# Expert routing moved from a stage of its own into the loop of the memory attention

## The reference

```python
def _L0_ffn_ref(x, router_w, w1, b1, w2, b2):       # E = 8 experts, C = 1536 places each
    logits = x_flat @ router_w.T
    probs = softmax(logits)
    chosen_e, chosen_p = argmax(probs), max(probs)
    onehot = one_hot(chosen_e, E)
    pos = cumsum(onehot, axis=0)[token, chosen_e] - 1     # over all 8192 tokens, in order
    kept = pos < C
    buf[chosen_e, clip(pos)] += x_flat * kept             # then the experts' two products on buf
    y = eo[chosen_e, clip(pos)] * chosen_p * kept
x = x + _L0_xattn_ref(_layernorm(x), ctx_1024, ...)   # "memory attention": 16 heads of 64,
                                                      # keys of 128 tokens and 77 memories
x = x + _L0_ffn_ref(_layernorm(x), ...)
```

## Time and profile before

| | us |
|---|---|
| median of 3 runs (lowest, highest) | 3627.68 (3622.21, 3630.70) |
| the profiled execution: its own time | 3633.43 |
| its span, from the first to the last instruction | 3631.6 |
| busy in the span: PE, DVE, ACT, POOL | 3202.6, 2524.3, 2207.0, 1508.8 |
| mean granted clock of PE | 0.929 of full |

### The profile page before, as it was taken

One profiled execution on the slowest core, in us unless ns is written; L12 is line 12 of the kernel. 1 busy time (PEld: TensorE's weight loads), 2 busy tenths in 40 slices (PEclk: granted clock), 3 DMA queues, 4 the chain that ended last, 5 costly groups with the idle time before them and its releaser, 6 DMA issues. The chain is left out here.

```text
span 3631.6 us, 96279 instructions
## 1 busy us (share of the span) xinstructions
PE 3202.6 (88%) x27249; PEld 2343.7 (65%) x27249; DVE 2524.3 (70%) x7783; ACT 2207.0 (61%) x8571; POOL 1508.8 (42%) x2416
## 2 busy tenths in 40 slices
PE   8999999899999999999999731887996999977776
PEld 4656565788888888888888520665664666644444
DVE  7888888676777777777767640114666888879997
ACT  6888888566666666666666300334776999962221
POOL 6888888111111111111111125004654777746665
PEclk9999999999999999999999855999998999986666
DMA  4000000000000000000000101321000000000000
GB/s 138 0 0 0 0 0 1 4 2 3 2 2 2 2 2 2 2 2 2 2 2 2 70 9 50 84 77 30 17 16 5 6 5 5 6 3 6 12 12 18
DMA packets 80357, 54.27 MB, mean 15 GB/s; under 512 B 24801, under 2 KB 74413, under 8 KB 80160
## 3 DMA queue, kind: packets, MB, share of 16 engines
q1 hardware_dynamic: 76192, 45.27, 4.4%
q0 software_dynamic: 4096, 8.16, 0.8%
HBM read 32.67 MB, written 20.97 MB: 15 GB/s over the span
## 5 line engine op out<-in xcount | busy, mean ns | idle before, releaser
L785 DVE COPY b_prT<-b_tr 128x512 f32<-128x512 f32 x512 | 352.4, 688 | 324.3 <-PE b_tr L694 320.6
L930 POOL TENSOR_TENSOR b_ln_var<-b_ln_mean_var,all_eps 128x1 f32<-128x1 f32 x64 | 12.2, 190 | 1158.5 <-DVE b_ln_mean_var L129 1158.5
L883 ACT ACTIVATE b_pr<-b_sc,b_low 128x205 f32<-128x205 f32 x1024 | 431.2, 431 | 40.9 <-DVE b_low L761 40.9
L467 ACT ACTIVATE a_pr<-a_sc,a_low 128x128 f32<-128x128 f32 x1024 | 365.5, 384 | 36.4 <-POOL a_pn L511 26.2
L776 DVE TENSOR_SCALAR b_pn<-b_pr,b_rec 128x205 f32<-128x205 f32 x1024 | 291.6, 327 | 54.7
L694 PE MATMUL b_tr<-all_ident,b_pn 128*128 128x128 f32 x2048 | 322.4, 280 | 6.2 <-DVE b_prT L785 2.5
L2064 ACT ACTIVATE f_pr<-f_sc,f_low 128x77 f32<-128x77 f32 x1024 | 320.3, 338 | 10.2 <-DVE f_low L1955 2.9
L502 POOL TENSOR_TENSOR a_kx<-a_qk,w_hsel 128x512 f32<-128x512 f32 x256 | 291.8, 1151 | 2.4 <-DVE a_qk L338 2.4
L694 PEld LDWEIGHTS b_tr<-all_ident,b_pn 128*128 128x128 f32 x2048 | 226.5, 141 | 92.2 <-issue 69.5
L254 PE MATMUL a_sc<-a_kx,a_qk 128*128 128x512 f32 x512 | 261.9, 593 | 0.0
L761 DVE TENSOR_REDUCE b_low<-b_sc 128x4 f32<-128x820 f32 x256 | 256.3, 1001 | 6.0 <-PE b_sc L682 6.0
(11 more groups left out here) (290 smaller groups left out, 8651.3 us busy)
## 6 DMA issues: line engine op xcount, KB each, us to landing
scratch_x<-r_zeros SPq DMA_DIRECT2D x12, 512.0 KB, 5.0
e_xr<-scratch_x SPq DMA_DIRECT2D x24, 256.0 KB, 3.0
scratch_y<-e_yr SPq DMA_DIRECT2D x24, 256.0 KB, 2.4
all_X<-in_x SPq DMA_DIRECT2D x8, 512.0 KB, 7.0
e_w<-in_e_w SPq DMA_DIRECT2D x16, 256.0 KB, 3.0
out_x<-all_X SPq DMA_DIRECT2D x8, 512.0 KB, 3.2
w_mask<-in_mask SPq DMA_DIRECT2D x1, 2464.0 KB, 9.8
b_cT<-in_ctxT SPq DMA_DIRECT2D x32, 77.0 KB, 1.9
```

The lines of the kernel that those rows point to most:

```text
L467: op = act.activation(pr[:, u % 2, g], sc[:, u % 2, 128 * g:128 * g + 128], ACT.Exp, bias=low[:, u % 2, g:g + 1], scale=-1.0, accum_out=su ...
L785: dve.tensor_copy(prT[:, j % 2, i].rearrange("p h t q -> p (h t q)"), tr[:]).then_inc(prT_made, 1)
L883: op = act.activation(pr[:, j % 2, g, 0:KN], sc[:, j % 2, h, KN * i:KN * i + KN], ACT.Exp, bias=low[:, j % 2, g:g + 1], scale=-1.0, accum_ ...
```

## The change

The routing's stage is gone. Its work is done inside the memory attention, for two sequences at a time, some steps behind them. The expert stage itself is the same. What is added to the loop, by engine:

- DVE: after the residual of sequence b - 1 its statistics (part 1) and its normalised rows into XN (part 2), in every step. In odd steps `find_least` (end of part 1) and `choose` (end of part 3) for sequences b - 3 and b - 2; in even steps `settle` (end of part 1) for b - 4 and b - 3.
- PE: four kinds of chunks in the ring. Even sequences' chunks get lg (logits of two sequences); odd ones get place (counts, in bf16) and two rT (transposes of XN). The ring has now 14 and 12 chunks, and xT of an even sequence stands ahead of mk2.
- ACT: the copies of those chunks, and `weigh`, two exponentials with their sums, in odd steps.
- POOL: in every step the root of the routing's norm; in even steps a wait for `settle` and two indirect DMAs.
- SP: the twelve stores of zeros stand between the first and the second load of the context.

The loop's body is four steps instead of two (`over_fours`), since the four slots of XN and the two halves of `put` go round with four sequences. After the last step the last four sequences are routed in straight code.

```diff
-        CHUNKS = [[("mk", 0), ("mk", 1), ("mk", 2), ("mk", 3), ("xT", 0), ("q", 0), ("k", 0), ("q", 1), ("k", 1),
-                   ("mv", 0), ("v", 0), ("v", 1), ("mv", 1)],
-                  [("xT", 0), ("q", 0), ("k", 0), ("q", 1), ("k", 1), ("mv", 0), ("v", 0), ("v", 1), ("mv", 1)]]
-        EARLY = [[[0, 1], [3, 4, 5], [7], [10]], [[0], [], [4], []]]
-        LATE = [[[2], [6], [8, 9], [11, 12]], [[1], [2, 3], [5, 6], [7, 8]]]
+        CHUNKS = [[("mk", 0), ("mk", 1), ("xT", 0), ("mk", 2), ("lg", 0), ("mk", 3), ("q", 0), ("k", 0), ("q", 1),
+                   ("k", 1), ("mv", 0), ("v", 0), ("v", 1), ("mv", 1)],
+                  [("xT", 0), ("q", 0), ("place", 0), ("k", 0), ("q", 1), ("k", 1), ("mv", 0), ("v", 0), ("v", 1),
+                   ("mv", 1), ("rT", 0), ("rT", 1)]]
+        EARLY = [[[0, 1], [4, 5, 6], [8], [11]], [[0], [], [5], []]]
+        LATE = [[[2, 3], [7], [9, 10], [12, 13]], [[1, 2], [3, 4], [6, 7], [8, 9, 10, 11]]]
...
 PE
+                def router_logits(n, dst):
+                    if due(n):
+                        pe.wait_ge(pj_copied, n)
+                    for i in range(2):
+                        last = pe.matmul(dst[:, E * i:E * i + E], rT[:, i], rwT[:], start=True, stop=True)
+                def count(s, dst):
+                    pe.wait_ge(choosing, 4 * s + 8)
+                    pe.wait_ge(placing, 3 * s)
+                    pe.matmul(dst[:, 0:2 * E], ones_bf[:], earlier[:].unsqueeze(1).broadcast_to([128, 2, E]), start=True, ...)
+                    pe.matmul(dst[:, E:2 * E], ones_bf[:], one_hot[:, 0], start=False, stop=False)
+                    return pe.matmul(dst[:, 0:2 * E], tri_bf[:], one_hot[:]..., start=False, stop=True)
...
 DVE
+                def choose(s):
+                    dve.wait_ge(weighed, s + 2)
+                    dve.tensor_reduce(top[:], hit[:], AX.X, ALU.max).then_inc(choosing, 1)
+                    dve.wait_ge(choosing, n + 1)
+                    dve.tensor_tensor(hit[:], hit[:], per_token(top), ALU.is_equal).then_inc(choosing, 1)
+                    dve.wait_ge(choosing, n + 2)
+                    dve.tensor_tensor(hit[:], hit[:], per_expert(rank), ALU.mult).then_inc(choosing, 1)
+                    dve.wait_ge(choosing, n + 3)
+                    dve.tensor_reduce(best[:], hit[:], AX.X, ALU.max).then_inc(choosing, 1)
+                    dve.reciprocal(chance[:], total[:]).then_inc(choosing, 1)
+                    dve.wait_ge(choosing, n + 5)
+                    dve.tensor_tensor(one_hot[:], hit[:], per_token(best), ALU.is_equal).then_inc(choosing, 1)
+                    dve.tensor_tensor(chance[:], chance[:], top[:], ALU.mult).then_inc(choosing, 1)
+                    dve.wait_ge(choosing, n + 7)
+                    dve.tensor_tensor(both[:], one_hot[:, 0], one_hot[:, 1], ALU.add)
+                    dve.tensor_tensor(chosen_base[:], one_hot[:], per_expert(base), ALU.mult).then_inc(choosing, 1)
+                def settle(s, h, copied):      # nine instructions, four waits for the one before, then put
...
                     for j in range(NJ):
+                        if j == 1 and inside(b - 1):
+                            dve.wait_ge(y_added, b)
                         copy_probs(b, j, 0)
+                        if j == 1 and inside(b - 1):
+                            route_statistics(b - 1, 1 - p)
...
                             divide(nb, nj, 1)
-                        if j == 0 and not (isinstance(b, int) and b == 0):
-                            residual(b - 1)
+                        if inside(b - 1):
+                            if j == 0:
+                                residual(b - 1)
+                            if j == 1:
+                                dve.wait_ge(r_seen, b)
+                            if j == 2:
+                                route_normalise(b - 1, (r + 3) % 4)
+                        if routed and p == 1 and j == 1:
+                            find_least(b - 3, ...)
+                        if routed and p == 1 and j == 3:
+                            choose(b - 3)
+                        if routed and p == 0 and j == 1:
+                            settle(b - 4, r // 2, chunk_end(b + 1, 1, "place", 0))
+                        if inside(b - 1):
+                            if j == 1:
+                                dve.bn_aggr(r_mv[:, 1 - p], r_stats[:, 1 - p]).then_inc(r_moments, 1)
...
 ACT, part 3 of odd steps, ahead of copy_out
+                def weigh(s):
+                    for i in range(2):
+                        act.activation(hit[:, i], minus[:, i], ACT.Exp, bias=least[:, i:i + 1], scale=-1.0,
+                                       accum_out=total[:, i:i + 1]).then_inc(weighed, 1)
...
 POOL
                     add_bias(b)
                     if not isinstance(b, int) or b + 2 < B:
                         both_norms(b + 2, p)
+                    if routed and p == 0:
+                        pool.wait_ge(placing, 3 * b - 6)
+                    if inside(b - 1):
+                        route_norm(b - 1, 1 - p)
+                    if routed and p == 0:
+                        scatter(r // 2)
...
 SP
                 load(0)
+                sp.wait_ge(zeroed, 3)
+                for n in range(rows.shape[0]):
+                    sp.dma_start(rows[n], zeros[:]).then_inc(buf_zeroed, 16)
                 with sp.Fori(1, B // 2) as j:
                     load(j)
```

More of the change, by code:

```diff
@@ L84, in over_sequences, with over_fours @@
         step(b, b % 2, b == n - 1)
+def over_fours(eng, step, n, head, tail):
+    for b in range(head):
+        step(b, b % 4)
+    with eng.Fori(head // 4, (n - tail) // 4) as j:
+        for r in range(4):
+            step(4 * j + r, r)
+    for b in range(n - tail, n):
+        step(b, b % 4)
 def wait_for_loads(nc, loaded, pairs):
@@ L720, in project_out, with step @@
                     last.then_inc(y_made, 1)
-                def step(b, p, last):
-                    first = isinstance(b, int) and b == 0
+                def step(b, r):
+                    p = r % 2
+                    first, last = isinstance(b, int) and b == 0, isinstance(b, int) and b == B - 1
+                    half = ((r + 2) % 4) // 2
                     for j in range(NJ):
@@ L751, in _ @@
                 score(0, 0, 1)
-                over_sequences(pe, step)
+                over_fours(pe, step, **steps)
+                for i in range(1, 6):
+                    after(i)
             @block.vector
@@ L800, in step @@
+                def step(b, r):
+                    p = r % 2
+                    last = isinstance(b, int) and b == B - 1
                     ahead = not isinstance(b, int) or b + 2 < B
+                    routed = not isinstance(b, int) or b >= 3
                     for j in range(NJ):
@@ L920, in _ @@
                 exponentials(0, 0, 1)
-                over_sequences(act, step)
+                over_fours(act, step, **steps)
+                for i in range(1, 5):
+                    after(i)
+                weigh(B - 2)
+                after(5)
             @block.gpsimd
@@ L1203, in stage_experts, with no_weights @@
-def stage_experts(nc, w, consts, buf, answers):
+                pool.wait_ge(buf_zeroed, 16 * rows.shape[0])
+                over_fours(pool, step, **steps)
+                pool.wait_ge(placing, 3 * B - 6)
+                scatter(0)
+                route_norm(B - 1, 1)
+                pool.wait_ge(placing, 3 * B)
+                scatter(1)
+                for n in range(4):
+                    pool.wait_ge(scattered[n], 4 * B)
+def no_weights(mem, w):
+    return (), []
+def stage_experts(nc, X, w, consts, tiles):
```

426 lines of the change are left out of this document (188 added, 238 removed).

## The result

The changed kernel takes 3585.06 us (median of 4 runs, 3575.12 to 3589.88) against 3627.86 (4 runs): a ratio of 0.9873, 95% interval 0.9859 to 0.9888, clear of 1. The profiled execution is the fastest of the four: 3575.12 us, span 3573.3. Its span is 58.3 us shorter. The stretch between the stages gave 177.8, and 132.3 of them went back into the memory attention. The experts and the silu attention took 1.7 less.

What follows compares the result with a forecast made beforehand. PE was taken to bound the memory attention, 43.4 us a pair. Of 174.8 us saved between the stages, 113 return (31 pairs at 3.65), leaving 61.8: 3571.6 for the profiled execution, 3566 as median, range 3495 to 3612.

Steps and rivals of the forecast that it cites:

- The saving between the stages: Between memory attention and experts: of the 201.0 us there, 174.8 are saved after tail, start and clock.
- PE's idle ahead of T(0,1): Sign in even steps of the loop: new idle time of PE there on b_prT, about 1.3 us.
- rival 2: Loop's body of four steps no longer stays in instruction memory: 14 passes at 3.8 us, 53 us, 3619; chance 0.08.
- tail: After the last residual, routing the last four sequences until the experts' first load: 27 us, bounds 16 and 40.
- the experts' clock: Experts start some 27 us after busy work instead of cold: 0 to 8 us won, taken as 3.
- The start: PE's start waits for five more memsets and the cast of tri: 2.2 us, bounds 0 and 4.
- PE's passes: PE's added loop work per pair: rT 1.0, logits 0.5, counts 0.4, moving xT gains 0.25; sum 1.65 us.
- DVE's pieces: Routing work on DVE ahead of copies PE awaits: choose 1.3, settle 0.6, route_normalise 0.1; 2.0 us per pair.
- Half as many loop branches: 0: Memory attention's loop: going from two to four steps a body, with half the branches, changes the time by 0.
- Rival 3: Computed waits in the loop cost DVE 0.44 us instead of 0.10: 62 us slower, 3690; chance 0.04.
- Rival 1: DVE's pieces fit in the slack, only PE's passes and ring waits show: 1.65 a pair, 3504; chance 0.20.
- Rival 4: Port lock: two scatters hold DVE up to 1.9 us a pair, 60 us; 3600 if half hidden; chance 0.04.

Runs made afterwards that it cites:

- e1: The changed kernel with the memory attention's 64 steps written out straight on all four engines: 3537.1 us, ratio 0.9738 to the kernel before.
- e8: The changed kernel with the steps written out on DVE alone, the other engines keeping the loop: 3541.7 us, ratio 0.9751 to the kernel before.
- e7: The changed kernel with the steps written out on PE alone, the other engines keeping the loop: 3595.8 us, ratio 0.9891 to the kernel before.
- e6: The kernel before, without the routing in its loop, with the steps written out on all engines: 3634.5 us, ratio 1.0016 to the kernel before.
- e2: The kernel before with four steps in the loop's body instead of two, no routing in it: 3633.3 us, ratio 1.0006 to the kernel before.
- e12: The changed kernel with the steps written out on DVE and ACT, PE and POOL keeping the loop: 3553.9 us, ratio 0.9780 to the kernel before.
- e4: The changed kernel with rT and v1 reordered in the ring and even sequences' q(0) not waiting for mk3's copy: 3544.3 us, ratio 0.9770.
- e13: The changed kernel with steps written out on all engines and even sequences' q(0) not waiting for mk3's copy: 3501.2 us, ratio 0.9633.
- e11: The changed kernel with steps written out on all engines, rT and v1 reordered, q(0) not waiting for mk3's copy: 3493.2 us, ratio 0.9612.

## Why the prediction was right, and where it was not

Forecast 3566, range 3495 to 3612, faster: measured 3585.06. The saving between the stages came true by its mechanism. The size of the loop's cost came true by luck: inside it a term 38 us too large met a loss of 49 us that had been put at nothing. Of the signs that were named, the stretch stayed under 30 us, PE's idle ahead of T(0,1) came (0.69 in e1, not 1.3), and so did the sign of rival 2, idle "issue" once per four steps.

- **The stretch.** A tail of 27 was forecast, 23.2 measured: the hand-overs overlap a little more. The experts and the silu attention together took 1.7 us less, where 3 were forecast for the experts' clock. Right.
- **The start.** Forecast 2.2, measured 10.1 (the first addition to X moved from 684.8 to 694.9). PE starts 2.7 us later, at 647.36 instead of 644.63. Then, by its timeline, it waits 1.2 for the normalised rows at 650.97, since xT now stands ahead of mk2, and does a chunk of logits (1.0) that isn't needed yet; and it stays at half clock longer. How the rest divides among these was not tried. Its windows, before and after:

```profile
650.00:655.00 5.00, 4.70 (x37) 4.42 (x38) 0.84 (x2) 2.82 (x5) 1.34 (x4) 1.00 0.08 16
```

```profile
650.00:655.00 5.00, 3.43 (x13) 2.99 (x13) 1.07 (x4) 1.31 (x4) 2.40 (x9) 0.50 1.02 403
655.00:660.00 5.00, 4.39 (x23) 4.16 (x22) 0.48 (x1) 1.37 (x3) 0.00 (x0) 0.55 1.02 405
```

- **PE's passes.** Forecast 1.65 a pair. By the rows: rT 1.25 (1.0 forecast), logits 0.37 (0.5), counts 0.08 (0.4: the three bf16 products start 0.03 apart), q(0) against xT -0.1 (-0.25): 1.6.
- **DVE's pieces: the step that was mis-sized.** Forecast 2.0 a pair. Without the branch, by e1, the routing costs (1439.7 - 1366.6)/31 = 2.36 in all, so DVE is left with 0.76, nearly all of it the 0.69 that T(0,1) waits for `choose` in e1. `choose` lasts 1.35, not 1.8 (an instruction that waits starts 0.20 after the one before, one that doesn't 0.09), and `settle` fits into its slack of 1.4. That is 38 us over 31 pairs too many.
- **"Half as many loop branches: 0" failed.** Rival 2 had the mechanism, as far as the runs show it (a stall at each branch back of this body), at 49 us by e1 where it was priced at 53, with a chance of 0.08. Its reasoning went wrong in one place: the stalls of PE and DVE don't simply add to 3.8 a pass. Together they cost 3.5; with DVE's gone 0.9 of it was left (e8), with PE's gone all of it and more (e7). The Trainium skill, "Runtime: NRT & Kernel Launch" (Instruction fetch mechanics), says that a taken branch to a target outside the window held stalls on a fetch, while straight code is fetched ahead. e1 and e6 agree with that: no such stall without a branch. e2 has a branch and no stall, so by that rule its body would still be held; no run here measures what an engine holds.
- **Rival 3** (computed waits at 0.44) was wrong: between small operations that wait for each other lie 0.19 to 0.21 us in e1 and 0.19 to 0.29 in the loop. **Rival 1** supposed a loop cost of 1.65 a pair: in straight code it would have been 2.36, between it and the forecast. **Rival 4**: the hold is real, but at most some 9 us by the rows above, not up to 60, since it lasts only from an operation's start to the scatter's end. The row that the sum went by the earlier trace rows was of another operation. The Trainium skill, "SBUF — State Buffer" (the section on the two sides of SBUF), gives the shared ports to whoever starts first for the whole instruction and blocks the other, and limits this on DVE's side to 2-port modes and to two inputs in SBUF, which the prediction left out. The ends of the held products, 0.04 to 0.06 us behind the scatter's, agree with the first part; PSUM reads were not held at all.
- **The range.** The bounds of the terms as listed add up to 0.65 and 7.3 us a pair, not 1.2 and 7, and 2.4 a pair gives 3527, not 3530. Neither would have moved the measured time out of the range.

By terms: loop 122 for 113, start 10 for 2, tail 4 less, clock 1 more: some 14 of the 19 us between forecast and median. The other 5 are within the 15 us over which the four runs spread. In the profiled execution the 11.1 us of the last stages hid most of the 14: forecast 3571.6, measured 3575.1.

## What to carry to other kernels

When a change makes a loop's body longer, compare the packets of the instruction queues and the idle time "issue" once per pass, before anything else; if they appear, write out the loop of the engine that the others wait for; writing out only that of PE, which waited, won nothing here. When chunks are put in another order, read each wait again for what it guarded: one that had become needless cost half as much as the fetches. Small work on an engine with spare time costs only what exceeds the slack of the copy that it stands ahead of; that slack is read from the timeline, and here it swallowed most of them.

## Not expected of the hardware

- Short idles halve PE's clock in the middle of a loop. 13 of 13 idles of 3.75 to 4.02 us did it in e7; of those of 1.8 to 2.6 us some did (one of 13 branches in the changed kernel, three in e8, four in e12, five in e4) and most did not. e1, with no idle over 1.1 us on PE, keeps 1.00 in its steady part. So repairing one engine's stall alone lengthened the profiled loop.
- The clock of the last stages falls differently from run to run, and by kernel: e13's four runs show means of 0.956 to 0.957, e11's five 0.948 to 0.951. The windows from 1000 to 1150 us behind the last addition to X, e1 and e13, whose work there is the same:

```profile
3134.40:3284.40 150.00, 99.34 (x357) 59.95 (x355) 125.65 (x452) 33.62 (x111) 77.10 (x136) 0.64 0.03 7
```

```profile
3108.80:3258.80 150.00, 94.61 (x373) 56.29 (x373) 129.55 (x470) 34.94 (x115) 80.50 (x142) 0.73 0.03 7
```

The end of the kernel lies 1400.8 us behind that addition in e1 and 1390.2 in e13. What decides it was not tried.
- Straight code moved 163 packets of instructions in the window and showed no idle "issue" above 1.3 us. Which size of the body is the limit on each engine stays open: by e2 and the changed kernel between 643 and 673 instructions on PE, 327 and 415 on DVE, 227 and 252 on ACT, if size alone decides.
